# First attention of a two-block decoder: heads outermost, scores on two row halves, values on two column halves

## The reference

```python
x = x + L0_attn(ln(x), qkv_kernel, qkv_bias)                    # the part that is changed
x = x + L0_xattn(ln(x), ctx, Wq, bq, Wk, bk, Wv, bv)            # one head of 128
x = x + L0_ffn(ln(x), gate_w, w1, b1, ..., sw1, ...)            # 8 experts, top 2, and a shared one
x = x + L1_attn(ln(x), A, B, C, gamma, beta)                    # a linear recurrence over 64 positions
x = x + L1_xattn(ln(x), ctx, mask, W_q, W_k, W_v, W_o, b_o)     # 8 heads of 64
x = x + L1_ffn(ln(x), Wg, W1, W2)                               # 8 experts, each takes its top 128 tokens

def L0_attn(inputs, qkv_kernel, qkv_bias):      # 16 heads, causal
    qkv = einsum('bse,ef->bsf', inputs, qkv_kernel) + qkv_bias  # (16, 64, 384)
    qkv_heads = qkv.reshape(b, heads, s, -1)                    # (16, 16, 64, 24)
    q, k, v = split(qkv_heads, 3, axis=-1)                      # 8 features each
    qk = einsum('bhse,bhte->bhst', q, k) / sqrt(2 * 128)
    attn = softmax(qk + upper triangle of -inf, axis=-1)
    return einsum('bhst,bhte->bhse', attn, v).reshape(b, s, e)
```

## Time and profile before

| what | value |
|---|---|
| three runs | 270.34, 274.4, 275.8 us (median 274.4) |
| profiled execution | span 267.4 us from first to last instruction; its own device time is not listed apart |
| TensorE, VectorE, ScalarE, GpSimd busy | 94%, 70%, 55%, 31% of the span |
| mean granted TensorE clock | 0.994 of full |
| chain that ended last | TensorE 76%, VectorE 9%, transfers 5%, ScalarE 4% |
| transfers | 11.64 MB, half of the packets under 512 B |

### The profile page before, as it was taken

One profiled execution on the slowest core, in us unless ns is written; L12 is line 12 of the kernel. 1 busy time (PEld: TensorE's weight loads), 2 busy tenths in 40 slices (PEclk: granted clock), 3 DMA queues, 4 the chain that ended last, 5 costly groups with the idle time before them and its releaser, 6 DMA issues.

```text
span 267.4 us, 5236 instructions
## 1 busy us (share of the span) xinstructions
PE 251.2 (94%) x1842; PEld 174.3 (65%) x1842; DVE 186.4 (70%) x628; ACT 146.3 (55%) x303; POOL 83.7 (31%) x139
## 2 busy tenths in 40 slices
PE   8999899999898999999999768899998999999995
PEld 8663588867665656766675423667986566777775
DVE  4458696799765846476324997668566588889975
ACT  0566665552655587787756335464735944443550
POOL 7733994001010446456765131083331000000000
PEclk9999999999999999999999997999999999999999
DMA  5799900033711000000000000000000000000002
GB/s 143 156 311 251 270 16 2 0 78 101 215 29 53 1 0 0 2 1 0 2 1 1 0 2 0 2 0 2 5 5 0 0 0 4 0 0 2 0 1 81
DMA packets 21991, 11.64 MB, mean 44 GB/s; under 512 B 10968, under 2 KB 20957, under 8 KB 21965
## 3 DMA queue, kind: packets, MB, share of 16 engines
q1 hardware_dynamic: 20925, 10.94, 15.0%
q0 software_dynamic: 80, 0.20, 0.7%
q10 hardware_dynamic: 960, 0.16, 0.3%
HBM read 8.68 MB, written 2.62 MB: 42 GB/s over the span
## 4 chain that ended last, share of the span: by engine, by line
PE 76%; DVE 9%; DMA 5%; ACT 4%; issue 3%; POOL 1%; POOLq 0%; SPq 0%; DVEq 0%
PE bank L1007 10%; PE bank L995 9%; PE bank L884 6%; PE bank L865 5%; PE bank L859 5%; PE bank L764 4%; PE bank L921 3%; PE bank L942 3%; PE bank L743 3%; PE bank L632 3%; PE bank L642 2%; DMA v_scratch<-QKVT 2%; PE bank L667 2%; PE bank L750 2%; PE bank L902 2%
## 5 line engine op out<-in xcount | busy, mean ns | idle before, releaser
L514 POOL TENSOR_TENSOR X<-X,att 128x128 f32<-128x128 f32 x72 | 30.1, 454 | 20.0 <-ACT att L1439 20.0
L440 POOL TENSOR_TENSOR rs<-rs,halves 128x4 f32<-128x4 f32 x14 | 14.3, 1020 | 69.0 <-DVE rs L1696 65.8
L995 PE MATMUL bank<-XT,Wb 128*128 128x512 f32 x64 | 30.0, 600 | 0.7 <-ACT XT L1293 0.7
L1007 PE MATMUL bank<-Wb,att 128*128 128x128 f32 x224 | 27.1, 277 | 0.0
L1007 PEld LDWEIGHTS bank<-Wb,att 128*128 128x128 f32 x224 | 26.1, 192 | 1.4 <-issue 1.4
L1479 ACT ACTIVATE att<-bank 128x512 f32<-128x512 f32 x32 | 18.7, 599 | 8.7 <-PE bank L995 8.5
L1439 ACT ACTIVATE att<-bank,comb 128x128 f32<-128x128 f32 x72 | 20.2, 379 | 4.1 <-PE bank L884 4.1
L1873 DVE SCALAR_TENSOR_TENSOR att<-bank,cols,att 128x512 f32<-128x512 f32 x18 | 13.5, 750 | 11.7 <-ACT att L1428 6.6
L884 PEld LDWEIGHTS bank<-W2a,att 128*128 128x128 f32 x144 | 17.9, 192 | 4.1 <-issue 2.9
L884 PE MATMUL bank<-W2a,att 128*128 128x128 f32 x144 | 18.7, 276 | 0.0
L865 PE MATMUL bank<-XT,W3a 128*128 128x512 f32 x36 | 18.1, 598 | 0.3 <-DVE att L1873 0.3
(11 more groups left out here) (230 smaller groups left out, 513.6 us busy)
## 6 DMA issues: line engine op xcount, KB each, us to landing
Wb<-in_L_ffn_W SPq DMA_DIRECT2D x1, 1024.0 KB, 5.2
Wb<-in_L_ffn_W SPq DMA_DIRECT2D x8, 128.0 KB, 4.8
X<-in_x SPq DMA_DIRECT2D x2, 256.0 KB, 3.2
k_scratch<-QKVT SPq DMA_DIRECT2D x1, 512.0 KB, 3.1
q_scratch<-QKVT SPq DMA_DIRECT2D x1, 512.0 KB, 2.8
Wb<-k_scratch SPq DMA_DIRECT2D x1, 512.0 KB, 4.5
v_scratch<-QKVT SPq DMA_DIRECT2D x1, 512.0 KB, 5.4
V<-q_scratch SPq DMA_DIRECT2D x1, 512.0 KB, 6.2
```

Source lines behind the costliest of these rows:

```text
L440: nc.gpsimd.tensor_tensor(rs[:, 0, cut], rs[:, 1, cut], halves[:, :], ALU.pow).then_inc(l_root[h], 1)
L514: nc.gpsimd.tensor_tensor(X[:, h * HT + t, :], X[:, h * HT + t, :], part0[:, i % 2, t, :], ALU.add).then_inc(f_acc, 1)
L995: mm(bank[i % 4][:, :], W1b[:, e, f * P:(f + 1) * P], XT[:, half(h)], start=True, stop=True).then_inc(m_up, 1)
L1007: last = mm(bank[4 + h][:, t * P:(t + 1) * P], hid[:, e % 2, f, tile], W2b[:, e, f, :], start=(f == 0), stop=(f == F1 - 1))
```

## The change

The partitions of the projections become (e, c), and those of KH, QH and VH (head, e): the head is outermost, so the lower 64 partitions hold heads 0 to 7 and the upper ones 8 to 15. The stores now write through `by_head`, in pieces of 64 elements, and the loads read 4 KB for each partition. The biases of q, k and v are copied into the new order ahead of their transposes.

A score product uses 64 partitions. Four copies of the keys do in place of eight, since copy a serves head pair a of the lower half and of the upper half. `scores(m)` serves two batches (2m, 2m + 1) and gives two units: unit 2m + u2 is the partition half u2 for both batches. It makes two causal products and four of 64 rows x 256 columns, with the two halves in different banks; four banks (0 to 3) hold scores, one (4) the transposes, two (5, 6) the weighted values. There are again 16 units of 128 x 512 scores.

`weigh_values(u)` makes eight products with 64-column weights and 18 columns in place of four of 128 and 34; the even head of a pair goes to output partitions 0 to 63, the odd one to 64 to 127, so `normalise` is one product on 128 partitions. VD has one copy of v (ScalarE the early batches, GpSimd the late ones), eight transposes and four copies (two on ScalarE, two on VectorE) make Vb, whose entries have 9 columns each (8 features and the one). `subtract_max` and `normalise` are split (`row_max`, `inverse`). Cross-attention of half 1 stays in bank 6 and that of half 0 goes to bank 7. All hand-written lists are re-ordered; `add_states` has its steps joined, and `mask_row`, one pass over 1024 columns for the last attention, goes from the first attention to the first experts.

```diff
-    VW = 2 * HD + 1
-    VN = 2 * VW
+    VW = HD + 1
+    NP4 = 4
+    NM = B // 2
+    NU = B
...
-        KB = big[:, 8 * N:].rearrange("p (a n k) -> p a n k", a=NPAIR, k=S)
+        KB = big[:, 8 * N:12 * N].rearrange("p (a n k) -> p a n k", a=NP4, k=S)
...
-                return qkv_d[s].rearrange("(c e) (h x) -> e h c x", e=HD, x=S).rearrange("e h c x -> (e h) c x")
+                return qkv_d[s].rearrange("(h e) (c x) -> e c h x", e=HD, x=S).rearrange("e c h x -> (e c) h x")
             def store(s, copied, stored):
                 sp.wait_ge(copied, 2)
-                sp.dma_start(qkv_d[s], QKVT[:, s, :]).then_inc(stored, 16)
+                sp.dma_start(by_head(s), QKVT[:, s, :].rearrange("p (h x) -> p h x", x=S)).then_inc(stored, 16)
             def load(s, stored, dst, loaded):
                 sp.wait_ge(stored, 16)
-                sp.dma_start(dst.rearrange("p (c x) -> p c x", x=S), by_head(s)).then_inc(loaded, 16)
+                sp.dma_start(dst, qkv_d[s]).then_inc(loaded, 16)
...
+            for a in range(NP4):
                 widen_keys(a)
             pool.wait_ge(ld_qh, 16)
             for g2 in range(2):
                 nc.gpsimd.tensor_scalar(late(QA[:, :, g2, :]), QH[:, HB:B, :, :], evens[:, g2:g2 + 1], None, ALU.mult
                                         ).then_inc(kb_late, 1)
-                pool.wait_ge(kb_late, NPAIR + 1 + g2)
+                pool.wait_ge(kb_late, NP4 + 1 + g2)
+            pool.wait_ge(ld_vh, 16)
+            nc.gpsimd.tensor_copy(VD[:, HB:B, :, :], VH[:, HB:B, :, :]).then_inc(vd_late, 1)
...
+            pe.wait_ge(c_bias, 1)
+            nc.tensor.transpose(bank[4][:, 0:31], vecs[:, :], ident[0:31, 0:31])
+            nc.tensor.transpose(bank[4][:, 31:34], biases[:, :], ident[0:3, 0:3]
+                                ).then_inc(prep_psum, 1)
...
+                pe.wait_ge(v0_ready, 2)
+                pe.wait_ge((vd_early, vd_late)[g], 1)
                 for i in range(4):
-                    last = nc.tensor.transpose(bank[4 + g][:, i * P:(i + 1) * P],
-                                               VD[:, 4 * g + i, :, :].rearrange("p r a -> p (r a)"), ident[:, :])
+                    n = 2 * (4 * g + i)
+                    last = nc.tensor.transpose(bank[6 + g][:, i * P:(i + 1) * P], VD[:, n:n + 2, :, :].rearrange("p n c t -> p (n c t)"), ident[:, :])
...
+            def scores(m):
+                if m == 0:
                     pe.wait_ge(c_misc, C_MISC)
                     pe.wait_ge(prep_act, 5)
-                    pe.wait_ge(pow_ready, 1)
-                if n == 2:
+                if m == 1:
                     pe.wait_ge(kv_ready, 2)
                     pe.wait_ge(kv_dve, 2)
-                if n == HB:
-                    pe.wait_ge(kb_late, NPAIR + 2)
-                if n >= 3:
-                    pe.wait_ge(a_sub, n - 2)
-                dst = bank[n % 3]
-                mm(dst[:, :], perm[:, :], causal[:, :, :].rearrange("p a k -> p (a k)"), start=True, stop=False)
-                if n == 0:
-                    pe.wait_ge(kb_early, NPAIR)
+                if m == NM // 2:
+                    pe.wait_ge(kb_late, NP4 + 2)
+                if m >= 2:
+                    pe.wait_ge(a_sub, 2 * m - 2)
+                for u2 in range(2):
+                    rows = slice(u2 * S, (u2 + 1) * S)
+                    mm(bank[2 * (m % 2) + u2][:, :], perm[rows, :], causal[rows, :, :].rearrange("p a k -> p (a k)"),
+                       start=True, stop=False, skip_group_check=True)
+                if m == 0:
+                    pe.wait_ge(kb_early, NP4)
                     pe.wait_ge(qa_early, 2)
-                mm(dst[:, :], QA[:, n, :, :].rearrange("p g a -> p (g a)"), KB[:, :, n, :], start=False, stop=True).then_inc(a_scores, 1)
-
-            def transpose_probs(n):
-                pe.wait_ge(a_exp, n + 1)
-                if n >= 1:
-                    pe.wait_ge(a_trc, n)
-                for p4 in range(4):
-                    last = nc.tensor.transpose(bank[3][:, p4 * P:(p4 + 1) * P],
-                                               Es[:, n % 3, p4 * P:(p4 + 1) * P], ident[:, :])
+                for n2 in range(2):
+                    for u2 in range(2):
+                        rows, n = slice(u2 * S, (u2 + 1) * S), 2 * m + n2
+                        dst = bank[2 * (m % 2) + u2][:, :].rearrange("p (a n k) -> p a n k", n=2, k=S)
+                        last = mm(dst[:, :, n2, :], QA[rows, n, :, :].rearrange("p g a -> p (g a)"), KB[rows, :, n, :],
+                                  start=False, stop=True, skip_group_check=True)
+                        if n2 == 1:
+                            last.then_inc(a_scores, 1)
+
...
+            def weigh_values(u):
+                pe.wait_ge(a_trc, u + 1)
+                if u == 0:
+                    pe.wait_ge(vb_act, 2)
+                if u == HB:
+                    pe.wait_ge(vb_dve, 2)
+                if u >= 2:
+                    pe.wait_ge(a_norm, u - 1)
+                if u == 9:
+                    pe.wait_ge(o_act[0], 1)
+                for p4 in range(NP4):
+                    for g2 in range(2):
+                        head = (u % 2) * 2 * NP4 + 2 * p4 + g2
+                        last = mm(bank[5 + u % 2][g2 * S:(g2 + 1) * S, p4 * 2 * VW:(p4 + 1) * 2 * VW],
+                                  PTs[:, u % 2, p4 * P + g2 * S:p4 * P + (g2 + 1) * S],
+                                  Vb[:, u // 2, head, :, :].rearrange("p n v -> p (n v)"), start=True, stop=True)
...
+            act.wait_ge(ld_vecs, 128)
+            AF(biases[:, :].rearrange("s (e c) -> s e c", c=CH), vecs[0:3, :].rearrange("s (c e) -> s e c", e=HD), ACT.Copy
+               ).then_inc(c_bias, 1)
...
+            def align_values():
                 act.wait_ge(ld_vh, 16)
-                AF(VD[:, :, 1, :].rearrange("p n (c t) -> p n c t", t=GT), VH, ACT.Copy).then_inc(vd_act, 1)
+                AF(VD[:, 0:HB, :, :], VH[:, 0:HB, :, :], ACT.Copy).then_inc(vd_early, 1)
 
...
+            def inverse(u):
+                dve.wait_ge(a_pv, u + 1)
+                V.reciprocal(rO[:, u, :].rearrange("p (a n) -> p a n", n=2), weights(u)[:, :, :, HD]).then_inc(a_inv, 1)
+            def normalise(u):
+                dve.wait_ge(a_inv, u + 1)
+                m, u2 = u // 2, u % 2
+                first = 2 * (m % (NM // 2))
+                V.tensor_tensor(
+                    Opos[:, m // (NM // 2), u2 * NP4:(u2 + 1) * NP4, :, first:first + 2].rearrange("p a e n -> p a n e"),
+                    weights(u)[:, :, :, 0:HD],
+                    rO[:, u, :].rearrange("p (a n) -> p a n", n=2).unsqueeze(3).broadcast_to([P, NP4, 2, HD]), ALU.mult
+                    ).then_inc(a_norm, 1)
+            def row_max(u):
+                dve.wait_ge(a_scores, u + 1)
+                V.tensor_reduce(mx0[:, u, :], bank[u % 4][:, :].rearrange("p (a s) -> p a s", s=S), AX.X, ALU.max
+                                ).then_inc(a_max, 1)
+            def subtract_max(u):
+                dve.wait_ge(a_max, u + 1)
+                if u >= 3:
+                    dve.wait_ge(a_tr, u - 2)
+                V.tensor_tensor(Es[:, u % 3, :].rearrange("p (a s) -> p a s", s=S),
+                                bank[u % 4][:, :].rearrange("p (a s) -> p a s", s=S), per_row(mx0[:, u, :], S),
                                 ALU.subtract).then_inc(a_sub, 1)
...
             copy_xt(5, 1, 6)
-            copy_ys(0, 0)
             route_exp()
             gelu(0, 0, 1)
             gelu(0, 1, 1)
+            copy_ys(0, 0)
...
             probs1(7)
+            ln_moments(5, 0)
+            search_bits()
             add1(4)
-            ln_moments(5, 0)
             add1(5)
...
             keys_values1(10)
-            keys_values1(11)
-            keys_values1(12)
             transpose_xn(3, 1, 6)
             inject(1)
             widen(1, 0)
             widen(1, 1)
+            keys_values1(11)
             widen(1, 2)
             read_out(1)
+            keys_values1(12)
             keys_values1(13)
             keys_values1(14)
```

470 lines of the change are left out of this document (229 added, 241 removed).

## The result

| | before | changed |
|---|---|---|
| median of four executions | 272.37 us (270.0 to 275.8) | 268.18 us (265.92 to 270.48) |
| ratio | | 0.986, 95% interval 0.982 to 0.990 |
| span of the profiled execution, granted clock | 267.4 us, 0.994 | 268.4 us, 0.962 |

Forecast were 269.0 us and a gain of 5.4; the gain of the medians is 4.2. All ratios in this document leave out the executions that were slowest, mostly at a low TensorE clock; the profiled one of the changed kernel (0.962) is among those, and its two executions in the ratio, at clocks of 0.987 and 0.994, had spans of 264.7 and 264.0.

What follows compares the result with a forecast made beforehand. TensorE was taken to bound the first attention stretch, VectorE a close second, and a serial chain the second stretch. -3.5 - 0.9 - 0.5 - 0.5 = -5.4 us from 274.4 gave 269.0 us, 80% range 264.5 to 274.0.

Steps and rivals of the forecast that it cites:

- rival (a): In both attention stretches, waits between the engines eat most of the gain: -2.2 us, 272.2 us; chance 0.16.
- three signs of being wrong: Value product above 1 us, VectorE idle over 4 us between 25 and 49, or the expert stage growing.
- The first score stays at 24.1 + 0.3: Opening: q, k, v transfers leave the first score product at 24.1 us; only the biases add 0.3.
- rival (e): Opening: scattered stores cost 9.0 us, not 4.9, so first scores wait for q: -2.4 us, 272.0 us; chance 0.07.
- TensorE's prices: Attention: two units' scores cost 1.27 us, a value product 0.65; savings of 7.0 and 3.8 us of TensorE.
- First value product 8.1 us behind the first score: First stretch: the first value product comes near 32.5 us, four us sooner than before.
- VectorE sets the pace from there: First stretch: VectorE's 21.6 us of work from 25.5, plus 1.7 waiting, put output transposes at 48.8: -3.5 us.
- Second stretch -0.9: Output transposes to gate: cross-attention's products no longer queue behind late value products: -0.9 us, bounds 0 and -1.5.
- Rival (b): Second attention stretch: TensorE's clock falls with less work, 1 to 2 us on the chain: -3.9 us, 270.5 us; chance 0.12.
- Recurrence -0.5: Around the transposes at 148.12: fewer key/value products ahead, VectorE's order changed: -0.5 us, bounds +0.8 and -1.3.
- an expert stage that only hands on: First mixture of experts: TensorE-bound, it passes on the gate's gain of 4.4 us.
- Route -0.5: Routing: ScalarE's 0.6 us copy goes behind the exponential, the serial search starts sooner: -0.5 us, bounds 0 and -0.6.

Runs made afterwards that it cites:

- fillers: Changed kernel plus useless TensorE products in the waits around half 0's layernorm 1 and in half 1's recurrence: 267.25 us median, ratio 0.986 to the kernel before.
- the repeated run: The changed kernel as it is, measured and profiled once more: 271.65 us median, ratio 0.989 to the kernel before.

## Why the prediction came out as it did

Of the signs that the prediction named, the two prices came true and none of the times. The output transposes were at 51.73 (50.83 with fillers) and not at 48.8, behind the 50.5 that it gave for rival (a). The gate was at 81.5 (78.4) and not at 77.3. Two of its three signs of being wrong came true: VectorE is idle 5.9 us between 25 and 49 (4.6 in the repeated run), and the expert stage grew. By steps, with the kernel with both fillers beside the profiled one (us, in brackets the difference to before). The fillers' profile has full clock from 33 to 157 us, but 0.65 from 28 to 32 and 0.57 from 157 to 161:

| from ... to | before | changed | both fillers |
|---|---|---|---|
| first score at | 24.1 | 27.07 (+2.9) | 26.77 (+2.6) |
| to first value product | 12.2 | 8.8 (-3.4) | 8.2 (-4.0) |
| to output transposes | 15.9 | 15.8 (-0.1) | 15.8 (-0.1) |
| to addition | 9.1 | 8.5 (-0.7) | 8.5 (-0.6) |
| to gate | 20.3 | 21.3 (+1.0) | 19.1 (-1.2) |
| to VectorE's moments of half 1's layernorm 3 | 61.7 | 62.7 (+1.0) | 62.7 (+1.1) |
| to their transposes (148) | 4.8 | 3.8 (-1.0) | 3.8 (-1.0) |
| to the transposes of half 0's layernorm 4 | 10.3 | 14.1 (+3.8) | 10.9 (+0.6) |
| to the end | 109.0 | 106.3 (-2.7) | 107.9 (-1.1) |

The sums are +1.0 and -3.7; the second is what the ratio of 0.986 shows (-3.8 of 270).

1. *The first score stays at 24.1 + 0.3.* This step failed; it is at 26.7 to 27.1. I priced one scattered store and one contiguous load, 8.0 us in all. k's store did take 4.0, less than my 4.9. But q's store, beside k's, took 5.0 for 2.8, and no load became cheaper, k's 4.6 and q's 6.2 as before: 11.3 us for q where 9.2 stood in the trace (14.07 to 23.28). With the biases, 0.9 late and not 0.3, that is the 2.9. It was rival (e), by another mechanism than a doubled price. The Trainium skill, "DMA: Bandwidth & Descriptors", Specifications, has pieces under 512 bytes done as read-modify-write. The trace agrees in direction: the two stores took 6.9 us for 4.8, 1.44 times as long, though not twice.
2. *TensorE's prices.* Right: 1.18 for 1.27, 0.52 to 0.58 for 0.65; 7.7 and 5.0 to 5.9 us less where I had 7.0 and 3.8. The rule weighed there, a floor of some 60 cycles an instruction in the Trainium skill ("TensorEngine Tiling (Array Packing)", Performance Considerations), is 0.025 us as an estimate at 2.4 GHz. The sixteen narrow instructions take 0.03 each, so they do sit near that floor, which I had called not at work. Its conclusion fails all the same: a wide one costs 0.11.
3. *First value product 8.1 us behind the first score.* Right: 8.2, and 7.9 in the repeated run, at full clock.
4. *VectorE sets the pace from there.* Wrong, though its 16.3 us for this part came out at 15.8. TensorE sets it, and the part is as long as before. In the chain its eight value products cost 2.3 us less (4.4 for 6.6), but six units are scored in it and not three (+0.3), four value transposes (0.6) and the transposes of a sixth unit's probabilities (0.6) fall into it, the powers cost 0.3 more, and VectorE's piece at the end 0.3 more. The powers of the matrix, some 3 us of work without hurry, stand there in both. VectorE needed less than I took: parting maximum and subtraction does save (below).
5. *Second stretch -0.9.* Too small at full clock: -0.6 up to the addition and -1.2 behind it, more than the bound of -1.5; the profiled execution has +0.3. The chain up to the addition didn't go through store and load alone, as I read it: before, it stood in VectorE's maxima and subtractions of half 1 from 54.44 on, and the transfer was ready at the same time. Now it is the transfer's, whose store takes 3.2 for 3.5. This is from the chain before:

```profile
59.14 0.69 DVE Es L1811
```

Behind the addition, four value products of half 1 stood in the chain before the cross-attention's values (0.81 to 1.01 each); two are left (0.48 and 0.58).
6. *Rival (b), the clock falls there.* It came true in both profiles of the changed kernel, with +1.0 and +3.0 from addition to gate where full clock gives -1.2. I gave it 0.12, and took the recurrence's clock as it was.
7. *Recurrence -0.5, and an expert stage that only hands on.* VectorE's part, from the application of one layernorm to that of the next, is 10.87 for 11.24: -0.4. The transposes at 148 stand 1.0 closer to their moments, as forecast. But the stage ahead of them grew by as much, from the gate (81.68, and then 81.48) to the moments:

```profile
143.36 0.87 DVE L1683 BATCH_NORM_STATS2 stats<-X 128x6 f32<-128x128 f32 x4
```

```profile
144.19 0.87 DVE stats L1699 x4
```

It is 62.7 us in the repeated run too. The chain was TensorE's from 87.9 to 141.8 before; now it leaves it from 93.4 to 100.7, for ScalarE and VectorE. What holds it there was not tried. At half clock the products moved behind the recurrence hold the next transposes for 3.3 us; 2.7 of the 3.8 us come back later, since they are work that has to be done anyway.
8. *Route -0.5.* Nothing. The counts of VectorE, before and then changed (the two rows ahead are a unit's maximum and the next one's):

```profile
25.28 0.69 DVE L1808 TENSOR_REDUCE mx<-bank 128x8 f32<-128x512 f32 x1 [0.32 <-PE bank L743]
...
26.61 0.68 DVE L1808 TENSOR_REDUCE mx<-bank 128x8 f32<-128x512 f32 x1
...
211.90 0.36 DVE L1977 TENSOR_REDUCE cnt<-bank 128x24 f32<-128x192 f32 x1 [0.81 <-PE bank L1034]
```

```profile
212.89 0.36 DVE L1997 TENSOR_REDUCE cnt<-bank 128x24 f32<-128x192 f32 x1 [1.41 <-PE bank L1062]
```

The layernorm ahead of it starts at 203.78 and 204.76 (the shifts of the earlier trace rows stood one us behind the first). Behind it the exponential comes 0.6 sooner (5.55 and 4.96), and the first count, for which VectorE now waits 1.41 and not 0.81, no sooner: 8.12 and 8.13. It is queued on TensorE behind work of the experts. The rest, 55.5 us, is equal.

That the time was near (269.0 for 268.18) is largely luck. Of the 3.5 us forecast for the first stretch 0.5 came, 1.4 with fillers; of the 3.7 us that the kernel with both fillers gains, 1.8 lie in the second stretch (0.9 forecast) and 1.1 in the last row of the table, where I had named only the route, and which no run explains. The base moved too: the kernel before has a median of 272.37 with its fourth execution, not 274.4. I kept a distance of 7.0 us between profiled span and median; 1.7 of it lie outside the span, and the rest was executions at lower clock, of which the changed kernel has its own.

## What to carry to other kernels

Price a chain of transfers from all that share the engines at that time: of each, read issue and landing in the trace, not its price alone. Before a wait is shifted, look at what the next engine has queued ahead of the released work: ScalarE's one copy of v held a whole softmax. Relief for TensorE in a stretch that waits on a chain of small steps can cost its clock there; work without hurry, or fillers, belongs into the waits. Check a stage that is taken as a mere carrier by its own two ends: here it lost 1.0 us that the next step seemed to win.

## What the runs showed of the chip beyond that

- An f32 product of 64-column weights and 18 columns costs 0.032 us an instruction when neighbours use different column halves (1.04 for 32), and 0.042 when they don't (1.35); with 128-column weights and 36 columns 0.12 (1.91 for 16). On two row halves the order hardly matters: 0.86 and 0.97 for eight instructions.
- Two maxima and two subtractions on different banks, pair by pair, take 2.5 us, 1.2 a unit (the chain's 1.27 and 1.20); maximum and subtraction of one unit by turns took 1.33 (25.28 to 26.61). That is 2 us over 16 units, which the prediction put at nothing.
- Two scattered 512 KB stores in 256-byte pieces, k's issued at 13.1 to 13.2: whether q's followed 1.2 or 1.9 us behind, q's ended at the same time, 20.1.
